# A decoder layer on one core: each causal mask on GpSimd made by two instructions of two heads instead of one of four

## The reference, cut to what matters

```python
x = _layernorm(x + _L0_attn_ref(x, W_q, W_kv, W_o))          # products of Fourier-transformed heads
x = _layernorm(x + _L0_xattn_ref(x, ctx_2048, ctx_2048))     # the second, masked attention
x = _layernorm(x + _L0_ffn_ref(x, weight, rram_variation))   # ternary inputs times weights

scores = jnp.einsum('bhqd,bhkd->bhqk', qh, kh) / math.sqrt(hd)
causal = ki <= qi
scores = jnp.where(causal[None, None], scores, MASKED_BIAS)
attn = jax.nn.softmax(scores, axis=-1)
out = jnp.einsum('bhqk,bhkd->bhqd', attn, vh)
```

## Time and profile before

| | |
|---|---|
| time, median of 3 runs | 154.84 us (152.98 to 155.96) |
| profiled execution, its own time | 154.16 us |
| its span, first to last instruction | 152.4 us |
| granted TensorE clock, mean | 0.993 |
| busy: PE, DVE, ACT, POOL | 135.7, 131.9, 115.5, 100.5 us |
| instructions on POOL | 212 |

### The profile page before, as it was taken

How to read it: one execution, slowest core, us unless ns; L and a number is a source line. 1 busy time by engine, 2 the same in 40 slices (tenths; PEclk the granted TensorE clock), 3 DMA queues, 4 the chain that set the end, 5 groups by cost and what they waited for, 6 DMA issues and landing times.

```text
span 152.4 us, 4763 instructions
## 1 busy us (share of the span) xinstructions
PE 135.7 (89%) x1737; PEld 91.5 (60%) x1737; DVE 131.9 (87%) x420; ACT 115.5 (76%) x318; POOL 100.5 (66%) x212
## 2 busy tenths in 40 slices
PE   6999999999999799999999989999897988996540
PEld 2944657455674447766575856776675867674330
DVE  0036999999989699998999989999998999999972
ACT  3126655777694687979998999989999799978940
POOL 4020252536856457757989789799999889998542
PEclk9999999999999999999999999999999999999997
DMA  3897962231159404453283226845469951202212
GB/s 101 269 245 263 308 227 42 102 77 63 39 148 237 138 0 137 123 158 75 36 224 105 52 52 137 282 127 176 106 201 125 178 144 22 69 4 69 75 69 71
DMA packets 25208, 19.33 MB, mean 127 GB/s; under 512 B 13152, under 2 KB 21088, under 8 KB 25184
## 3 DMA queue, kind: packets, MB, share of 16 engines
q1 hardware_dynamic: 25184, 19.02, 47.5%
HBM read 14.16 MB, written 2.10 MB: 107 GB/s over the span
## 4 chain that ended last, share of the span: by engine, by line
PE 42%; DVE 22%; POOL 9%; SPq 7%; ACT 6%; issue 6%; DMA 5%; POOLq 0%
PE p L823 11%; DVE x L2101 8%; PE p L877 5%; PE p L843 5%; PE p L870 4%; POOL probs L418 4%; DMA x1T_b<-x_b 3%; PE p L897 3%; SPq L198 3%; POOL rstd L412 3%; PE p L829 3%; PE p L794 2%; ACT probs L1462 2%; PE p L799 2%; PE p L853 2%
## 5 line engine op out<-in xcount | busy, mean ns | idle before, releaser
L418 POOL TENSOR_SCALAR_AFFINE_SELECT probs<-probs 128x512 f32<-128x512 f32 x64 | 41.2, 663 | 8.6 <-ACT probs L1462 7.9
L2101 DVE TENSOR_REDUCE x<-p 128x4 f32<-128x512 f32 x64 | 41.7, 679 | 2.3 <-PE p L853 2.3
L1462 ACT ACTIVATE probs<-p 128x512 f32<-128x512 f32 x64 | 34.9, 602 | 4.3 <-PE p L870 4.2
L823 PE MATMUL p<-w_in,xT_s 128*128 128x512 f32 x64 | 30.2, 601 | 0.0
L412 POOL TENSOR_TENSOR rstd<-ve,power 128x1 f32<-128x1 f32 x48 | 27.6, 577 | 2.8
L1480 ACT ACTIVATE dev<-r,neg 128x256 f32<-128x256 f32 x41 | 21.0, 515 | 2.4 <-DVE neg L2074 2.4
L877 PE MATMUL p<-probs,vals 128*32 128x128 f32 x512 | 19.5, 278 | 0.7 <-ACT probs L1462 0.3
L870 PE MATMUL p<-x1T,keys 32*128 32x128 f32 x512 | 18.8, 283 | 1.0 <-ACT yT_s L1450 0.4
L870 PEld LDWEIGHTS p<-x1T,keys 32*128 32x128 f32 x512 | 15.7, 186 | 5.7 <-DVE x L2101 2.1
L407 POOL TENSOR_SCALAR ve<-spread 128x1 f32<-128x1 f32 x48 | 10.2, 212 | 13.1 <-ACT dev L1480 10.0
L823 PEld LDWEIGHTS p<-w_in,xT_s 128*128 128x128 f32 x64 | 11.4, 190 | 10.2 <-issue 9.1
(11 more groups left out here) (81 smaller groups left out, 252.2 us busy)
## 6 DMA issues: line engine op xcount, KB each, us to landing
keys<-ctxK SPq DMA_DIRECT2D x16, 256.0 KB, 3.6
vals<-ctxV SPq DMA_DIRECT2D x16, 256.0 KB, 3.2
xT_s<-xT SPq DMA_DIRECT2D x16, 128.0 KB, 3.0
x_s<-x SPq DMA_DIRECT2D x16, 128.0 KB, 3.2
out<-res SPq DMA_DIRECT2D x16, 128.0 KB, 2.3
wq_s<-w_q SPq DMA_DIRECT2D x1, 256.0 KB, 2.7
wkv_s<-w_kv SPq DMA_DIRECT2D x1, 256.0 KB, 3.8
fv_s<-ffn_vT SPq DMA_DIRECT2D x1, 256.0 KB, 3.4
```

Source lines behind the costliest of these rows:

```text
L418: nc.gpsimd.affine_select(out=part, in_=part, compare_op=ALU.is_ge, fill=0.0, base=0, pattern=[[0, GH], [1, TOK]], channel_multiplier=-1). ...
L823: last = nc.tensor.matmul(p[PROJ[n]][:], xT_s[n % XR][:, g, :], w_in[:, g, :], start=(g == HALVES[0]), stop=(g == HALVES[1]))
L1462: nc.scalar.activation(probs[n % 2][:, c, :, :].rearrange("p g q -> p (g q)"), p[SCORES[n][c]][:], ACT.Exp, scale=HD ** -0.5).then_inc(exp ...
L2101: nc.vector.tensor_reduce(x1[n % X1R][:, c::GH, HD], p[APPROX[n][c]][:].rearrange("p (h k) -> p h k", h=GH), AX.X, ALU.max, negate=True).t ...
```

## The change

`mask(n, c)` goes over the four heads of c in two instructions. The first takes heads g = 0 and 1, the second g = 2 and 3, each 128 x 256 elements, in place as before. Only the second signals `masked[c]`; the increment of `mask_go` still stands once in front of the pair. The order of calls on every engine, the waits and the banks are as they were.

```diff
             def mask(n, c):

                 pool.sem_inc(mask_go, 1)
-                part = probs[n % 2][:, c, :, :]
-                nc.gpsimd.affine_select(out=part, in_=part, compare_op=ALU.is_ge, fill=0.0, base=0,
-                                        pattern=[[0, GH], [1, TOK]], channel_multiplier=-1).then_inc(masked[c], 1)
+                for g in range(0, GROUPS, GROUPS // 2):
+                    part = probs[n % 2][:, c, g:g + GROUPS // 2, :]
+                    last = nc.gpsimd.affine_select(out=part, in_=part, compare_op=ALU.is_ge, fill=0.0, base=0,
+                                                   pattern=[[0, GROUPS // 2], [1, TOK]], channel_multiplier=-1)
+                last.then_inc(masked[c], 1)
```

## The result

The changed kernel takes 159.59 us (median of 6 runs, 159.39 to 161.89) against 154.02 us for the kernel before on the same chip (median of 6): a ratio of 1.039, 95% interval 1.035 to 1.044, or 6.0 us (the two medians lie 5.6 us apart). The forecast was +4.3 us and 159.1 us. Single executions of any of these kernels can show a lower granted TensorE clock near the end, which adds up to about 1.8 us (3.4 us in the kernel with merged masks), so the ratios leave out the executions that this disturbed most, four of six for the merged masks, and traces are compared at points ahead of it.

What follows compares the result with a forecast made beforehand. From 98 to 138.5 us POOL's queue was taken as always filled: 32 x 0.14 = 4.5 us, less 0.4 of waits, up to 0.4 back, gives 4.3; 154.84 + 4.3 = 159.1 us, range 158.2 to 160.2 (chance 0.55).

Steps and rivals of the forecast that it cites:

- The fixed part: On POOL, each mask's second instruction adds a fixed cost of 0.14 us, with 0.03 to 0.20 as range.
- The memset's 0.03: Lower end of the cost on POOL: 0.03 us per mask, as one-element memsets follow each other, if hidden like that.
- The sign of 12 us more busy time on POOL: Expected in the changed trace: POOL's recorded busy time rises by some 12 us, more than it costs.
- The late stretch: From 98.3 to 138.5 us, 32 masks add 4.5 us on POOL; 4.3 us reach the last mask.
- POOL's 0.4 us of waits: POOL's waits from 98 to 138.5 us absorb at most 0.4 us, and up to 0.4 us comes back.
- The carry across the DMA transpose: The chain's detour, 112.11 to 117.25 us, does not reset POOL's lateness, 2.0 us by 120.8 us.
- The early stretch: From 35 to 98 us, 32 masks add 4.5 us to POOL, covered by PE and DVE: nothing on the path.
- The feedback rival: POOL's lateness reaches ACT and DVE earlier; masks from 71 us count: 6.7 us, 161.5 us; chance 0.18, shared with 0.20 per mask.
- The tail: After the last mask at 138.5 us there are no masks, so it stays 13.9 us long.
- A hidden fixed part: Rival on POOL's queue, 98 to 138.5 us: the second half costs 0.03 us, +0.6 us, 155.4 us; chance 0.12.
- only the last stretch counts: Rival: delay up to 120.8 us is taken up, only the last 16 masks count, 2.2 us, 157.1 us; chance 0.13.
- The rival of 0.20 us per mask: Rival on POOL: each split mask costs 0.20 us, giving 160.8 us; chance 0.18, shared with feedback.

Runs made afterwards that it cites:

- the kernel with merged masks: Kernel before with nine pairs of neighbouring masks of tiles 9 to 15 merged into instructions of eight heads, one counting semaphore: ratio 1.011, slower by 1.7 us.
- The moved comparisons: Comparisons of tiles 8 and 9 moved from POOL to VectorE: on the changed kernel 159.52 us, ratio 1.037; on the kernel before, ratio 1.005.
- the experiment on tile 3: Kernel before with only the four masks of tile 3 split, into four instructions each: 155.81 us, ratio 1.014.
- the kernel with tiles 8 to 15: Kernel before with only the masks of tiles 8 to 15 split, 32 of 64: ratio 1.026, +4.0 us.

## Why the prediction was right, and where it was off

- **The fixed part.** 0.14 us was forecast, 0.13 measured between undisturbed halves. The middle between the bounds was right and so was the choice of row: the type conversions, read start to start (0.13). Recorded durations gave 0.20, which is too much. The Trainium skill (Perfetto Trace Analysis, GPSIMD Engine Instruction) tells one to time GpSimd by start-to-start spacing and not by its spans, and the trace agrees: 0.13 by spacing, 2 x 0.41 - 0.64 = 0.18 by the records. The memset's 0.03 is real, but for memsets. The sign of 12 us more busy time on POOL did not come: it is 9.1, since busy time counts an overlap once.
- **The late stretch.** 32 x 0.14 = 4.5 us, of which 4.3 were to reach the last mask. From the first mask of tile 8 to the end of the last one it was 4.4 us in the changed kernel's trace. The terms behind it came out otherwise. The masks took 25.31 us instead of 20.58, 4.7 us more or 0.15 each, because of the stretched halves. POOL's 0.4 us of waits went and their time was gained in full, where the prediction had half of it come back; variances and roots took some 0.1 us more. That the two deviations of 0.2 us cancel is luck. The moved comparisons show that such time can come back: there a wait of 0.62 us opens that ends with work hanging on POOL's own masks. The carry across the DMA transpose held: tiles 12 to 15 alone gave 2.2 us of it, not all.
- **The early stretch is the step that failed.** "I cost it at nothing for the path" measured 1.3 us in the changed kernel, 1.1 us in the trace with only the early masks split, and 1.6 us timed. The prediction compared sums, 2.2 us of masks against 2.3 us of waits, and looked only from 71 us on. It missed the masks of tiles 2 and 3. At tile 3 the third mask ended 0.07 us ahead of its weighing in before; the experiment on tile 3 shows that hole. Positions of PE behind the weighings of tiles 2 and 3, before first, then changed, and the waits of the weight loads on masks from 35 to 98.3 us, before first:

```profile
61.68 0.66 PE L884 MATMUL p<-ident_s,outT_s 128*128 128x128 f32 x4
...
65.72 0.66 PE L860 MATMUL p<-ident_s,x 128*128 128x128 f32 x4
```

```profile
59.96 0.43 PE L879 MATMUL p<-probs,vals 128*32 128x128 f32 x8 [0.29 <-POOL probs L419]
...
61.42 0.66 PE L886 MATMUL p<-ident_s,outT_s 128*128 128x128 f32 x4
...
65.85 0.66 PE L862 MATMUL p<-ident_s,x 128*128 128x128 f32 x4
```

```profile
PEld p L877 <- POOL probs L418: 0.2, 1, 0.2
```

```profile
PEld p L879 <- POOL probs L419: 3.2, 6, 0.8
```

From 0.66 us early at the start PE comes to 0.26 early behind tile 2 and 0.13 late behind tile 3: 0.4 us each. The other 0.5 us, up to 0.61 late at tile 8, falls to tiles 4 to 7. It can't be told more closely than to 0.4 us, since the traces drift by as much there without any change. The feedback rival had priced that later part at 2.2 us, which was too much.
- **The tail** was forecast to stay as it was, 13.9 us; it is 14.1.
- **The rivals.** A hidden fixed part is excluded by the distances, and "only the last stretch counts" by the kernel with tiles 8 to 15. The measured +6.0 us lies between the forecast's +4.3 and the feedback rival's +6.7, inside the range. The rival of 0.20 us per mask gave +6.0 as well, but undisturbed distances show 0.13 and the whole late stretch 0.15. That 159.6 us lies so near to the forecast 159.1 is in part luck too: the forecast started from a median of 154.84 us, which is 154.02 with three more runs; as a ratio it said 2.8% and 3.9% was measured.

The working adds up to 4.4 + 1.3 + 0.2 = 5.9 us against 6.0 timed.

## What to carry to other kernels

The fixed part of a GpSimd instruction was best read from the distance between starts, since the records overlap, and it differs by kind (0.13 us for selects and type conversions, 0.03 for a memset); splitting costs that part for every piece on an engine with a full queue, however low its share of the whole span. Whether waits elsewhere cover it can't be told from their sum: look for the one consumer with no slack behind the operation. And where a wait ends with work that the same engine feeds, part of what it should absorb can come back, as the 0.62 us in the moved comparisons did.

## What the runs showed of the hardware

- GpSimd's select of float32 costs 0.13 us + 0.90 ns per element of a partition, start to start, from 128 to 512 elements; a memset of one element behind it adds 0.03 us. Between 98 and 144 us single halves lasted 0.45 to 0.63 us instead of 0.41, with open cause.
- In the tail TensorE can fall to the lower of its two clock levels (1.2 instead of 2.4 GHz). It stood idle for more than half of that time: it was busy 5.17 of 14.10 us in the changed kernel's tail (granted clock 0.89) and 6.55 of 15.30 in that of the kernel with tiles 12 to 15 split (0.71). Six matmuls of the last feed-forward of the changed kernel and of the one with tiles 12 to 15 split:

```profile
151.63 0.83 PE L899 MATMUL p<-w_ffn,xqT_s 128*128 128x256 bf16 x6 [0.48 <-ACT xqT_s L1473]
```

```profile
146.72 1.46 PE L900 MATMUL p<-w_ffn,xqT_s 128*128 128x256 bf16 x6 [0.48 <-ACT xqT_s L1474]
148.87 1.46 PE L900 MATMUL p<-w_ffn,xqT_s 128*128 128x256 bf16 x6 [0.48 <-ACT xqT_s L1474]
```

Two such groups, 0.63 us longer each, make 1.3 us at the very end. It came in some executions and not in others of the same kernel, so single runs of these kernels can't be compared to better than that.
